# Moving the additions of squares from GpSimd to VectorE in a Strassen-form attention and layer norm kernel

## The reference

```python
q = jnp.einsum('bnd,ed->bne', x, Wq)
k = jnp.einsum('bnd,ed->bne', x, Wk)
v = jnp.einsum('bnd,ed->bne', x, Wv)
rel = adjacency.T[None, :, :] * jnp.einsum('bnd,bmd->bnm', q, k)
rel = rel / jnp.linalg.norm(rel, axis=2, keepdims=True)
out = layernorm(x + jnp.einsum('bnm,bmd->bnd', rel, v))
```

## Time and profile before

| | |
|---|---|
| Median of 3 runs | 1965.12 us (1965.08 to 1965.24) |
| Profiled execution | 1964.93 us, of which the span of instructions 1963.1 us |
| Mean granted clock of TensorE | 0.999 |
| TensorE busy | 1952.8 us (99%), 9849 matmuls |
| VectorE busy | 1510.2 us (77%), 2091 instructions |
| ScalarE busy | 762.0 us (39%) |
| GpSimd busy | 926.9 us (47%), of it 320.7 us in the additions of squares |
| Transfers | 288.55 MB, mean 147 GB/s |

### The profile page before, as it was taken

One profiled execution on the slowest core, in us unless ns is written; L12 is line 12 of the kernel. 1 busy time (PEld: TensorE's weight loads), 2 busy tenths in 40 slices (PEclk: granted clock), 3 DMA queues, 4 the chain that ended last, 5 costly groups with the idle time before them and its releaser, 6 DMA issues.

```text
span 1963.1 us, 28669 instructions
## 1 busy us (share of the span) xinstructions
PE 1952.8 (99%) x9849; PEld 1666.3 (85%) x9849; DVE 1510.2 (77%) x2091; ACT 762.0 (39%) x1288; POOL 926.9 (47%) x633
## 2 busy tenths in 40 slices
PE   9999999999999999999999999999999999999998
PEld 6888888888888888888888888888888888888887
DVE  8886967869677796877968769687786877868775
ACT  5523534235242342423434243343333434335241
POOL 4545535464344643537444374452644536455352
PEclk9999999999999999999999999999999999999999
DMA  6444452434434344433344343434334343343501
GB/s 240 189 150 150 155 187 100 148 136 166 176 130 143 120 165 168 160 129 135 142 162 162 126 160 128 170 145 135 148 136 163 145 166 116 144 155 155 186 23 64
DMA packets 78544, 288.55 MB, mean 147 GB/s; under 512 B 7361, under 2 KB 7361, under 8 KB 74433
## 3 DMA queue, kind: packets, MB, share of 16 engines
q1 hardware_dynamic: 78528, 288.39, 40.2%
HBM read 247.46 MB, written 40.89 MB: 147 GB/s over the span
## 4 chain that ended last, share of the span: by engine, by line
PE 98%; DVE 1%; issue 1%; ACT 0%; POOL 0%; POOLq 0%; DVEq 0%
PE banks L422 33%; PE banks L424 32%; PE banks L423 32%; PE banks L430 0%; PE banks L438 0%; PE banks L442 0%; PE banks L446 0%; DVE yv L832 0%; DVE x_lo L768 0%; DVE aw L825 0%; DVE yv L941 0%; ACT yv L708 0%; DVE yv L973 0%; DVE v_raw L964 0%; DVE rel L926 0%
## 5 line engine op out<-in xcount | busy, mean ns | idle before, releaser
L422 PE MATMUL banks<-yv 128*128 128x512 f32 x1024 | 399.8, 390 | 0.5 <-DVE yv L941 0.5
L424 PE MATMUL banks<-yv 128*128 128x512 f32 x1024 | 398.5, 389 | 0.0
L423 PE MATMUL banks<-yv 128*128 128x512 f32 x1024 | 398.4, 389 | 0.0
L1158 POOL TENSOR_TENSOR square_sum<-square_sum,squares 128x512 f32<-128x512 f32 x224 | 320.7, 1432 | 90.0 <-ACT squares L673 79.4
L422 PE MATMUL banks<-yv,x_hi 128*128 128x512 f32 x896 | 348.8, 389 | 1.8 <-DVE rel L880 1.6
L424 PE MATMUL banks<-yv,x_lo 128*128 128x512 f32 x896 | 348.6, 389 | 0.0
L423 PE MATMUL banks<-yv,x_hi 128*128 128x512 f32 x896 | 348.6, 389 | 0.0
L1175 POOL TENSOR_TENSOR rstd<-var_eps,minus_half 128x1 f32<-128x1 f32 x128 | 145.4, 1136 | 318.3 <-DVE var_eps L1002 318.3
L423 PE MATMUL banks<-aw,x_hi 128*128 128x256 f32 x896 | 253.6, 283 | 0.0
L424 PE MATMUL banks<-aw,x_lo 128*128 128x256 f32 x896 | 253.5, 283 | 0.0
L422 PE MATMUL banks<-aw,x_hi 128*128 128x256 f32 x896 | 253.5, 283 | 0.0
(11 more groups left out here) (103 smaller groups left out, 3354.8 us busy)
## 6 DMA issues: line engine op xcount, KB each, us to landing
scr<-adj SPq DMA_DIRECT2D x128, 512.0 KB, 5.8
aw<-a_kept SPq DMA_DIRECT2D x15, 3584.0 KB, 11.1
aw<-w_kept SPq DMA_DIRECT2D x15, 3584.0 KB, 11.2
res<-x SPq DMA_DIRECT2D x128, 256.0 KB, 2.7
out<-res SPq DMA_DIRECT2D x128, 256.0 KB, 2.0
scr<-xT SPq DMA_DIRECT2D x30, 1024.0 KB, 7.1
a_kept<-aw SPq DMA_DIRECT2D x1, 3584.0 KB, 16.6
w_kept<-aw SPq DMA_DIRECT2D x1, 3584.0 KB, 11.2
```

The costliest lines, as they stand in the source:

```text
L422: pe.matmul(bank_ap, l_hi, r_hi, start=first and i == 0, stop=False, skip_group_check=on)
L423: pe.matmul(bank_ap, l_hi, r_lo, start=False, stop=False, skip_group_check=on)
L424: mm = pe.matmul(bank_ap, l_lo, r_hi, start=False, stop=i == len(pairs) - 1, skip_group_check=on)
L1158: pool.tensor_tensor(square_sum[:, h, :], square_sum[:, h, :], squares[:, n % SQRING, :], ALU.add).then_inc(square_added, 1)
```

## The change

`add_square` is defined on VectorE instead of GpSimd, with the same two waits and the same in-place addition. VectorE makes the 14 additions of a batch between its sums. In pair 0: m11 of tile 1 after the `s_r` sums, m22 of tile 1 after the mask of m21, and both m21 at the end (in the first batch these two come later, in pair 1). In pair 1: m12 of tile 0 and of tile 1 around the L901 of that pair, both m11 after `s_r`, both m22 after the mask of m21, both m21 at the end. The last two, m12 of tiles 2 and 3, come after the two L950 and before `chunk(b, 0)`. GpSimd keeps only the four masks of m22 in this stage. The number of additions, their order and the ring of two stay as they are. ScalarE, TensorE and SyncE are unchanged.

```diff
--- before.py
+++ after.py
@@ -881,6 +881,14 @@
                 for j in range(2):
                     y_lo_piece(b, B21, j, y_b21_raw[j])
 
+            def add_square(b, name, i):
+                n = added_order.index((name, i))
+                h = half_of[name]
+                dve.wait_ge(squared, b * SQUARES + (square_order.index((name, i)) + 1))
+                dve.wait_ge(square_added, b * ADDED + (n + SQRING))
+                dve.tensor_tensor(square_sum[:, h, :], square_sum[:, h, :], squares[:, n % SQRING, :],
+                                   ALU.add).then_inc(square_added, 1)
+
             def s_blocks(b, pair, first):
                 a, bb, c = (s_bank[pair][n] for n in ("a", "b", "c"))
                 tiles = (2 * pair, 2 * pair + 1)
@@ -892,6 +900,11 @@
                 if first and pair == 1:
                     wv_lo_piece(4)
                     wv_lo_piece(5)
+
+                    add_square(b, "m21", 0)
+                    add_square(b, "m21", 1)
+                if pair == 1:
+                    add_square(b, "m12", 0)
                 if pair == 0:
                     for j in range(2):
                         y_lo_piece(b, B22, j, y_b22_raw[j])
@@ -899,6 +912,8 @@
                     dve.wait_ge(adj_loaded[i], b * DMA + DMA)
                     dve.wait_ge(s_done, s_count(b, 2, i))
                     dve.tensor_tensor(c11(i), a[i % 2], adj_of(i, 0), ALU.mult).then_inc(s_m11, 1)
+                if pair == 1:
+                    add_square(b, "m12", 1)
                 if first and pair == 1:
                     wv_lo_piece(6)
                 for i in tiles:
@@ -908,6 +923,9 @@
                         dve.wait_ge(y_split[B22], b * 2 + (i + 1))
                     dve.wait_ge(s_done, s_count(b, 7, i))
                     dve.tensor_tensor(c22(i), c[i % 2], c21(i), ALU.add).then_inc(s_r, 1)
+                for i in tiles:
+                    if ("m11", i) not in firsts:
+                        add_square(b, "m11", i)
                 for i in tiles:
 
                     dve.wait_ge(s_r, b * HT + (i + 1))
@@ -925,6 +943,9 @@
                     dve.wait_ge(s_c21, b * HT + (i + 1))
                     dve.tensor_tensor(c21(i), c21(i), adj_of(HT + i, 0), ALU.mult).then_inc(s_m21, 1)
                 for i in tiles:
+                    if ("m22", i) not in firsts:
+                        add_square(b, "m22", i)
+                for i in tiles:
 
                     dve.wait_ge(s_u2, b * HT + (i + 1))
                     dve.wait_ge(s_done, s_count(b, 3, i))
@@ -935,6 +956,9 @@
                 for i in tiles:
                     dve.wait_ge(s_c12, b * HT + (i + 1))
                     dve.tensor_tensor(c12(i), c12(i), adj_of(i, 1), ALU.mult).then_inc(s_m12, 1)
+                if not (first and pair == 0):
+                    for i in tiles:
+                        add_square(b, "m21", i)
 
             def v_lo_piece(b, block, i, source):
                 dve.wait_ge(v_hi_made, b * 8 + (2 * V_BLOCKS.index(block) + i + 1))
@@ -1015,6 +1039,8 @@
                 s_blocks(b, 1, first)
                 v_sum(b, 6, 0)
                 v_sum(b, 6, 1)
+                add_square(b, "m12", 2)
+                add_square(b, "m12", 3)
                 chunk(b, 0)
                 v_lo_piece(b, (0, 0), 0, v_bank["a"][0])
                 v_lo_piece(b, (0, 0), 1, v_bank["a"][1])
@@ -1150,21 +1176,9 @@
                 pool.wait_ge(s_c22, b * HT + (i + 1))
                 pool.tensor_tensor(c22(i), c22(i), adj_of(HT + i, 1), ALU.mult).then_inc(s_m22, 1)
 
-            def add_square(b, name, i):
-                n = added_order.index((name, i))
-                h = half_of[name]
-                pool.wait_ge(squared, b * SQUARES + (square_order.index((name, i)) + 1))
-                pool.wait_ge(square_added, b * ADDED + (n + SQRING))
-                pool.tensor_tensor(square_sum[:, h, :], square_sum[:, h, :], squares[:, n % SQRING, :],
-                                   ALU.add).then_inc(square_added, 1)
-
             def s_blocks(b):
-                for name, i in square_order:
-                    if name == "m22" and i % 2 == 0:
-                        mask22(b, i)
-                        mask22(b, i + 1)
-                    if (name, i) not in firsts:
-                        add_square(b, name, i)
+                for i in range(HT):
+                    mask22(b, i)
 
             def power_norm(b):
                 pool.wait_ge(norm2_made, b + 1)
```

## The result

| | before | changed |
|---|---|---|
| Median | 1965.32 us (16 runs, 1965.08 to 1965.80) | 1969.45 us (16 runs, 1969.13 to 1969.97) |
| Ratio to before | | 1.0021, 95% interval 1.0014 to 1.0027 |
| Span of the profiled execution | 1963.1 | 1967.5 |
| A steady batch | 121.00 | 121.23 |
| VectorE / GpSimd busy | 1510.2 / 926.9 | 1576.6 / 606.6 |

What follows compares the result with a forecast made beforehand. The prediction took TensorE as the bound, held once per batch by a VectorE chain without slack. Steady batches 3.2 us plus first batch 0.4 made 3.6 us, forecasting 1968.7 us on the median's scale, range 1966.2 to 1973.5.

Steps and rivals of the forecast that it cites:

- TensorE hangs on L941 without slack: At each change from V products to outputs, TensorE waits for VectorE's chain from L979; moving L979 moves TensorE equally.
- The steady term, 0.22: Batch tail: two new additions take 1.32 us, pauses hide 1.10, leaving 0.22 a batch; 15 batches give 3.2 us.
- the replay: Step-by-step VectorE timeline computed for the changed kernel; in a steady batch it puts L979 at 935.57 against 935.35.
- The neighbour wait, 0.12: An addition waiting for its predecessor's semaphore starts 0.12 us later than a queued one, so a pair costs 1.32, not 1.20.
- The second L974 has a margin of about nothing: Second L950 (L974 after the change) keeps its start at 931.30; ScalarE's copy lets it go at 931.16 to 931.32.
- If L950 is ended by ScalarE's L693, rival 1 runs: Sign to check in the profile: ScalarE's copy L693, not TensorE, ends the wait of the second L950.
- rival 1: Ring of two makes ScalarE's copies delay the second L950; 0.6 more a batch gives 1977.5, half that 1973; chance 0.15.
- The first batch, +0.4: First batch, where VectorE also splits Wv without pauses: L979 at 88.75 against 88.36, +0.4 us, bounds -0.5 and +1.0.
- The masks' 2.35 us pay nothing: Four VectorE masks ahead of L950 shorten by 2.35 us without GpSimd's additions; four additions (2.64) spend it, no gain.
- Only place counts: VectorE load by itself costs nothing: additions in pauses are free, only those behind the second L950 cost, 0.22 a batch.
- Rival 4, faster: Tail starts earlier without GpSimd, winning at most the 0.18 gap at each change and 0.7 in the first batch: 1961.7; chance 0.04.

Runs made afterwards that it cites:

- before_op_at_turn: Kernel before, plus one unused VectorE instruction (bn_stats, 0.69 us) straight ahead of L979 in every batch; 1974.48 us, batch 121.60.
- pair_apart: Changed kernel with chunk 0's split placed between the two tail additions on VectorE; 1967.56 us, batch 121.11.
- extra_pair1: Changed kernel plus one unused VectorE instruction (bn_stats, step 0.60) in pair 1, behind the two L952, ahead of masks and m21 additions; 1978.11 us, batch 121.76.
- ring3: Changed kernel with a ring of three squares instead of two (SQRING 3); 1968.55 us, batch 121.23, first batch 56.66.
- extra_pair0: Changed kernel plus one unused VectorE instruction (bn_stats, step 0.60) in pair 0, behind the two L952; 1970.03 us, batch 121.23.
- before_chunk_later: Kernel before, with VectorE's second chunk split moved from between the two L960 to between the two L964; 1962.21 us, batch 120.83.

## Why the prediction came out as it did

The forecast was +3.6 us (1968.7), the measurement +4.1 (1969.45, or 1.0021, interval 1.0014 to 1.0027). The change lies just above the 0.2% that the text set as its line, the forecast just under it: the mechanism was right, and both terms of the sum, the steady batches and the first batch, were a little small.

- *TensorE hangs on L941 without slack.* Right; before_op_at_turn gives 0.60 for 0.60. Why the busy time hides the gap was read too simply. In TensorE's timeline of the kernel before, records of 0.28 start 0.12 apart, so they cover a start that is 0.10 late; the late product's record is longer too (0.47, where the ones after it have 0.39 to 0.40), and the next one starts 0.31 behind it where later ones start 0.23 to 0.24 behind. 0.10 and 0.08 make the 0.18:

```profile
945.31 0.28 PE L424 MATMUL banks<-aw,x_lo 128*128 128x256 f32 x1
945.53 0.47 PE L422 MATMUL banks<-yv 128*128 128x512 f32 x1
945.84 0.39 PE L423 MATMUL banks<-yv 128*128 128x512 f32 x1
```

- *The steady term, 0.22.* Right: 0.23. Each part is in the rows: an addition 0.69 long with a step of 0.60, its neighbour 0.72 behind it at the tail (1.41 for two), the two pauses used up, L1003 at 935.58 where the replay has 935.57. 15 x 0.22 is 3.3, which the prediction wrote as 3.2; what is missing to 3.5 is 0.01 a batch and the last batch, which takes 121.29.
- *The neighbour wait, 0.12.* Right in size at the tail of a looped batch, shown by pair_apart. But it isn't one size: at two of the five pairs of a looped batch (926.86 and 930.65) the second addition starts 0.79 behind the first (1.48 for two), 0.10 after the end of its predecessor and not the 0.04 of the earlier trace rows. In a looped batch these pairs are covered. In the first and the last batch, whose code stands outside the loop, the tail pair too has 1.48; in the last batch L1003 stands 0.05 later than in the others, which is most of its 0.06 over them:

```profile
1904.00 1.48 DVE L889 TENSOR_TENSOR square_sum<-square_sum,squares 128x512 f32<-128x512 f32 x2
```

- *The second L974 has a margin of about nothing.* Right: it keeps its place to 0.01, and the margin is about 0.06. The view names ScalarE as its releaser, but the 0.09 from the copy's end to its start, against 0.03 where the copy does end the wait, says TensorE. "If L950 is ended by ScalarE's L693, rival 1 runs" was too coarse a test. Rival 1's mechanism is real (extra_pair1: 0.53 of 0.60), but in a steady batch of the change it stays just short of acting (ring3: nothing to win there).
- *The first batch, +0.4.* The term that was mis-sized: 0.7. The replay put the second L950 at 84.48 and L979 at 88.75; they came at 84.89 and 89.23, of which 0.15 is the start of the program. The rest is 0.33. Most of it is about what the neighbour wait makes at 0.79 in place of 0.72: twice in the three additions at 66.60, once at 78.17 and once at the tail, four times 0.07; another 0.04 lies in ScalarE's steps from the first m21 addition to the second L974 (2.25 against 2.21). This is an estimate from the rows, not a run of its own. (The 1.47 that the prediction gave the first mask follows from none of its rows; that mask took 1.45.) ScalarE's copy behind the ring holds both L974 there, as the replay had it for the second, and three buffers take 1.0 us off. VectorE's timeline of the first batch:

```profile
78.17 1.48 DVE L889 TENSOR_TENSOR square_sum<-square_sum,squares 128x512 f32<-128x512 f32 x2
...
83.89 0.69 DVE L974 TENSOR_TENSOR v_raw<-banks,v_raw 128x512 f32<-128x512 f32 x1 [0.45 <-ACT v_raw L693]
84.89 0.69 DVE L974 TENSOR_TENSOR v_raw<-banks,v_raw 128x512 f32<-128x512 f32 x1 [0.31 <-ACT v_raw L693]
85.50 1.48 DVE L889 TENSOR_TENSOR square_sum<-square_sum,squares 128x512 f32<-128x512 f32 x2
...
89.23 1.30 DVE L1003 STREAM_TRANSPOSE squares<-square_sum 128x512 f32<-128x512 f32 x2
```

- *The masks' 2.35 us pay nothing.* Right that they bring no gain: L958 fell from 1291 to 684 ns, and the time didn't follow. But they are the room for the four additions ahead of the second L974. By extra_pair1 all but 0.06 of a delay there goes through, so without these 2.35 us those additions would have cost about 2.3 us a batch (an estimate; no run has the long masks with the additions on VectorE).
- *Only place counts.* Right: extra_pair0 and extra_pair1, the same instruction, 0.00 and 0.53 a batch.
- *Rival 4, faster.* The room it named, 0.18 at each change, was there, but the change couldn't reach it, since it touches nothing behind the second L950 for the better. before_chunk_later took it by moving another instruction: 0.17 a batch.

## What to carry to other kernels

An engine that the page shows as 99% busy may still hang on another at one point per loop turn: look for a weight load that stands further from its neighbour than the rest, and follow the waiting chain back to the last pause. Work in front of that pause is free up to the pause's length, provided that what ends the pause doesn't itself wait for that work (extra_pair0 against extra_pair1), and work behind it costs its full step times the number of turns; so ask of a move not how much load it brings to an engine but which pause pays for it. Where no pause covers them, put an independent instruction between two of which the second waits for the first (here 0.12 a turn). And read a releaser that the view names against its own end: it is the one only if the wait ends right behind it.

## What the runs showed of the hardware

A VectorE addition that waits for the semaphore of the addition straight ahead of it starts 0.72 or 0.79 us behind it, where a queued independent one starts 0.60 behind. Both sizes are stable to 0.01 from batch to batch and go by the place in the code: in the 14 looped batches 0.72 at three pairs (m21 of pair 0, m11 of pair 1, the tail) and 0.79 at two (926.86 and 930.65); in the first and the last batch, outside the loop, 0.78 to 0.80 at all of them. Why there are two sizes wasn't tried and stays open.

GpSimd's additions lengthened VectorE's masks, which have two SBUF inputs, to 1.14 and 1.29 us on the mean; without them the same lines take 0.70 and 0.68. No other large group of VectorE changed its length by more than 0.01. None of it shows as a gain in time; it is spent on the additions.
